# Routed experts on sorted tokens in blocks of 128 rows, in three of four chunks

## The chip, the cores and the metric

The kernel runs on one core of a Trainium2 chip. The metric is device time in microseconds (us) of one execution, all inputs in DRAM before and the output in DRAM after.

## The reference, cut to what matters

`x` is 16 sequences of 128 tokens of 128 features, `ctx` has the same shape. One decoder layer is computed in float32: 16-head self-attention with relative keys and values, causal cross-attention to `ctx`, and a mixture of experts, each followed by a residual add and a layer norm.

```python
x = _layernorm(x + _L0_attn_ref(x, ...))
x = _layernorm(x + _L0_xattn_ref(x, ctx_1024, ctx_1024, ...))
x = _layernorm(x + _L0_ffn_ref(x, ...))

def _L0_ffn_ref(hidden, router_w, router_b, sw1, sb1, sw2, sb2, rw1, rb1, rw2, rb2):
    flat = hidden.reshape(T, d)                                  # d = 128
    router_probs = jax.nn.softmax(flat @ router_w + router_b, axis=-1)     # 8 experts
    topk_probs, topk_idx = jax.lax.top_k(router_probs, 2)
    weights = jnp.zeros_like(router_probs).at[jnp.arange(T)[:, None], topk_idx].add(topk_probs)
    shared_out = jax.nn.gelu(flat @ sw1 + sb1, approximate=False) @ sw2 + sb2
    h1 = jax.nn.gelu(jnp.einsum('td,edh->teh', flat, rw1) + rb1[None], approximate=False)  # h = 256
    expert_out = jnp.einsum('teh,ehd->ted', h1, rw2) + rb2[None]
    mixed = jnp.einsum('ted,te->td', expert_out, weights)
    return (shared_out + mixed).reshape(b, s, d)
```

The weights are zero for all but 2 of 8 experts of a token, so three quarters of the routed products are multiplied by zero.

## The kernel before

The 16 sequences are taken in four chunks of 4, so a chunk is 512 tokens. For each chunk the work is cut into named steps: self-attention (`xT q k v bias p1 m p2 pv w2 pvT w2T X XT o ln`), cross-attention (`cT ck cv x1T cq c1 cm c2 cpv cpvT cX cXT co cln`), and the feed-forward part (`x2T r g up dn fln`). `st_` steps stack bf16 parts of queries and keys in SBUF by way of DRAM.

The order of all steps of all chunks is one list written out by hand in the text `SCHEDULE`. Every engine walks the same list and runs its own part of each step: TensorE (PE) the products, VectorE (DVE) and ScalarE (ACT) the reads from PSUM, GpSimd (POOL) the causal mask on the probabilities of `c2`, the residual bias and the `pow` of each layer norm, and SyncE (SP) the DMAs. Semaphores tie the engines together, so an engine that waits in one step holds back all its later steps. Steps of different chunks are interleaved: the feed-forward part of chunk 0 lies among the cross-attention of chunk 1 and the self-attention of chunk 2, and so on. The last chunk's feed-forward part has nothing beside it.

PSUM has two `ps_s` tiles of 128x1024 for scores and four `ps_f` tiles of 128x512 for all else, used in rotation. ACT computes both Exp (`p2`, `c2`, `r`) and Gelu (`up`); going from one to the other loads a table.

The feed-forward part is dense. `r` (L696, L993 to L1026) computes logits, softmax, and each expert's rank by a comparison of all pairs, and keeps the two highest as gate weights `gw`. `up` runs 18 times (9 experts, the shared one first, 2 halves of the hidden 256): one 512-column product from all tokens (L708), then Gelu on ACT (L833). `dn` runs 9 times: 8 products of 128 columns (L719), then DVE multiplies by the gate column and adds into `acc`, four instructions of 128x128 (L1044); the first `dn`, the shared expert's, adds `x2` and the output biases instead (L722, L1040). `fln` is the final layer norm and the store. All expert weights (2.1 MB) are loaded to SBUF at the start by `load_experts` (L374 to L386).

Of the kernel before, what the change touches and what calls it, by code (L numbers as in the profile page):

```python
# [15 lines left out]
BF16 = mybir.dt.bfloat16  # L16
ACT = mybir.ActivationFunctionType
# [23 lines left out]
NF = HID // P  # L41
NPC = 3
# [35 lines left out]
2xT 0cm.0 1pv.0 1p2.2 0c1.5 1p2.3 0c1.6 0c1.7 0c2.0 0cm.1 0c2.1 1p1.5 0c2.2 1pvT.0 1p1.6 0cpv.0 0c2.3 1pv.1
1p1.7 0cpvT.0 0c2.4 0cpv.1 0c2.5 1m.1 0c2.6 2q 2st_q 0c2.7 0cpv.2 1pvT.1 0cpvT.1 1p2.4 1p2.5 0cpvT.2 0cpv.3
1p2.6 1p2.7 1cv 2loadc 0cpvT.3 0cX 1pv.2 1ck 1w2.0 0cXT 2k 1w2.1 1pv.3 1w2.2 0co 0cln 1pvT.2 1w2.3 1pvT.3  # L80
2bias.0 1w2T.0 2bias.1 1w2T.1 1w2T.2 1w2T.3 1X 0x2T 2v 0r 1XT 2bias.2 2bias.3 1o 2bias.4 2bias.5 2st_k 0g
2bias.6 1ln 2bias.7 0up.0 2p1.0 0up.1 1x1T 2p1.1 0up.2 0up.3 1st_ck 3load 1cq 0up.4 0dn.0 2p1.2 0up.5 2p1.3
# [27 lines left out]


F_STEPS = {"xT", "q", "k", "v", "m", "pv", "w2", "pvT", "w2T", "XT", "o", "cT", "ck", "cv", "x1T", "cq", "cm",
           "cpv", "cpvT", "cXT", "co", "x2T", "r", "g", "up", "dn"}
# [969 lines left out]
```

## Time and profile before

| | us |
|---|---|
| median of 3 runs | 485.68 (484.39 to 485.95) |
| the profiled execution, whole | 484.97 |
| its span from first to last instruction | 482.9 |
| PE busy | 406.3 (84%) |
| DVE busy | 324.4 (67%) |
| ACT busy | 248.0 (51%) |
| POOL busy | 76.4 (16%) |

Busy time is the time in which an engine has an instruction in work; waits, and the issue of DMAs, are not in it. The granted clock is the share of 2.4 GHz that TensorE was given: 1.0 is 2.4 GHz, 0.5 is 1.2 GHz, and a mean between them is a mixture of the two in time. A float32 product appears as two matmul records.

### The profile page before, as it was taken

The numbers are of one execution on the slowest core, as the hardware profiler recorded it, in microseconds if no ns is written. First come the engines' busy times: TensorE is split into PE (matmuls) and PEld (weight loads), VectorE is DVE, ScalarE is ACT, GpSimd is POOL, SyncE is SP. The second block draws the span as 40 slices with busy tenths as digits, with TensorE's granted clock in tenths as the row PEclk, the third lists the DMA queues.
The fourth block names the chain that finished last, engine by engine and source line by source line (L and its number), as shares of the span: only waits on it lengthen the run. The fifth ranks groups of instructions, "written<-read, shape, count | busy, mean of one in ns | idle before, by whom it ended". The sixth has DMA issues, their size and how long they took to land.

```text
span 482.9 us, 11287 instructions
## 1 busy us (share of the span) xinstructions
PE 406.3 (84%) x4718; PEld 302.9 (63%) x4729; DVE 324.4 (67%) x630; ACT 248.0 (51%) x329; POOL 76.4 (16%) x84
## 2 busy tenths in 40 slices
PE   3775399847879999999899899998999998649992
PEld 2464158734656877767688676776786767525772
DVE  4429953698868787887787868888975377143233
ACT  2470187703558583368774932487973425514340
POOL 9700000201340120003411100113101102410000
PEclk9776589959999999999999999999999999876998
DMA  4558025140013513001121630011110200000001
GB/s 107 156 113 261 3 68 155 35 121 5 3 36 88 175 47 99 3 18 44 37 68 23 166 99 1 4 36 24 49 24 1 81 20 3 2 23 0 2 0 23
DMA packets 29324, 26.87 MB, mean 56 GB/s; under 512 B 12577, under 2 KB 27866, under 8 KB 28506
## 3 DMA queue, kind: packets, MB, share of 16 engines
q1 hardware_dynamic: 28442, 26.02, 20.0%
q8 instruction: 38, 0.62, 0.6%
q10 hardware_dynamic: 832, 0.13, 0.2%
q14 instruction: 12, 0.10, 0.1%
HBM read 18.38 MB, written 7.35 MB: 53 GB/s over the span
## 4 chain that ended last, share of the span: by engine, by line
PE 55%; DVE 22%; ACT 8%; DMA 5%; issue 4%; SPq 4%; POOL 1%; POOLq 0%; DVEq 0%; ACTq 0%
PE ps_f L708 12%; PE ps_f L719 11%; PE ps_s L545 8%; PE ps_f L571 5%; PE ps_f L671 3%; DVE ST L930 3%; DVE ST L960 3%; DMA QS<-MP 3%; PE ps_f L579 2%; ACT ST L786 2%; DVE MX L933 2%; PE ps_s L538 2%; PE ps_f L518 2%; PE ps_f L524 2%; SPq L414 2%
## 5 line engine op out<-in xcount | busy, mean ns | idle before, releaser
L545 PE MATMUL ps_s<-QS,KS 125*128 125x128 bf16 (+1 forms) x768 | 80.6, 249 | 16.7 <-DVE ST L930 11.2
L545 PEld LDWEIGHTS ps_s<-QS,KS 125*128 125x128 bf16 (+1 forms) x768 | 64.4, 106 | 43.9 <-issue 14.9
L833 ACT ACTIVATE HT<-ps_f,hb 128x512 f32<-128x512 f32 x72 | 48.9, 689 | 81.5 <-PE ps_f L708 39.2
L719 PEld LDWEIGHTS ps_f<-w,HT 128*128 128x128 f32 x576 | 69.2, 192 | 10.0 <-issue 7.4
L708 PE MATMUL ps_f<-x2T,w 128*128 128x512 f32 x144 | 73.5, 619 | 0.0
L719 PE MATMUL ps_f<-w,HT 128*128 128x128 f32 x576 | 73.3, 278 | 0.0
L790 ACT ACTIVATE ST<-ST 128x1024 f32<-128x1024 f32 x32 | 33.6, 1060 | 52.1 <-DVE ST L960 51.7
L1044 DVE SCALAR_TENSOR_TENSOR acc<-ps_f,gw,acc 128x128 f32<-128x128 f32 x128 | 37.4, 363 | 31.3 <-PE ps_f L719 31.2
L483 POOL TENSOR_SCALAR_AFFINE_SELECT PC<-PC 128x1024 f32<-128x1024 f32 x32 | 34.8, 1096 | 147.8 <-ACT PC L797 147.7
L930 DVE TENSOR_TENSOR ST<-ps_s,ST 128x1024 f32<-128x1024 f32 x32 | 38.6, 1207 | 13.4 <-PE ps_s L545 13.4
L937 DVE TRANSPOSE_TENSOR_REDUCE MX<-ps_s 128x32 f32<-128x1024 f32 x32 | 39.0, 1237 | 7.1 <-PE ps_s L545 7.1
L960 DVE TENSOR_TENSOR ST<-ps_s,ST 128x1024 f32<-128x1024 f32 x32 | 38.1, 1215 | 7.2 <-PE ps_s L554 7.0
L933 DVE TRANSPOSE_TENSOR_REDUCE MX<-ST 128x32 f32<-128x1024 f32 x32 | 39.8, 1245 | 1.1
L797 ACT ACTIVATE PC<-ps_s 128x1024 f32<-128x1024 f32 x32 | 32.5, 1026 | 14.2 <-PE ps_s L545 7.9
L489 POOL TENSOR_TENSOR ve<-mv,epst 128x4 f32<-128x4 f32 x12 | 2.4, 200 | 218.0 <-DVE mv L877 218.0
L708 PEld LDWEIGHTS ps_f<-x2T,w 128*128 128x128 f32 x144 | 25.0, 199 | 14.5 <-issue 13.5
L671 PE MATMUL ps_f<-ST,RV 128*8 128x64 f32 x1024 | 32.2, 290 | 0.1
L786 ACT COPY ST<-ps_s 128x1024 f32<-128x1024 f32 x32 | 30.6, 1028 | 3.0 <-PE ps_s L630 2.9
L671 PEld LDWEIGHTS ps_f<-ST,RV 128*8 128x8 f32 x1024 | 28.6, 107 | 3.7 <-issue 2.0
L554 PE MATMUL ps_s<-QS,onesr 128*128 128x512 bf16 x53 | 18.0, 415 | 14.5 <-DVE ST L930 5.1
L538 PE MATMUL ps_s<-maskT,identb 128*128 128x512 bf16 x64 | 26.1, 408 | 2.9 <-DMA QS<-parts_by_head 1.2
L805 ACT COPY OT<-ps_f 128x512 f32<-128x512 f32 x32 | 22.6, 709 | 7.7 <-PE ps_f L571 7.6
(114 smaller groups left out, 560.7 us busy)
## 6 DMA issues: line engine op xcount, KB each, us to landing
parts_by_head<-part SPq DMA_DIRECT2D x16, 384.0 KB, 2.7
QS<-parts_by_head SPq DMA_DIRECT2D x24, 256.0 KB, 3.8
KS<-parts_by_head SPq DMA_DIRECT2D x24, 256.0 KB, 4.9
xin<-in_x SPq DMA_DIRECT2D x16, 64.0 KB, 2.1
cin<-in_ctx SPq DMA_DIRECT2D x4, 256.0 KB, 4.5
w<-in_L_ffn_rw SPq DMA_DIRECT2D x1, 1024.0 KB
out_x<-acc SPq DMA_DIRECT2D x16, 64.0 KB, 1.8
QS<-MP SPq DMA_DIRECT2D x48, 8.0 KB, 2.1
```

What stands on the lines that cost most here:

```text
L538: nc.tensor.matmul(ps[:, half * BANK:(half + 1) * BANK], identb[:, :], maskT[:, :, :].broadcast_to([P, 4, S]), start=True, stop=False, ski ...
L545: last = nc.tensor.matmul(ps[:, o:o + S], KS[a][0:kd, c:c + S], queries(a, kd, h, j), start=not masked and j == 0, stop=j == NB - 1, skip_ ...
L671: last = nc.tensor.matmul(ps[a * QD:a * QD + HD, jj * HB:(jj + 1) * HB], RV[:, S - 1 - q, :], st_q[:, :, q, :], start=jj == 0, stop=jj == ...
L708: nc.tensor.matmul(ps[:, :], w1[:, e, f * P:(f + 1) * P], x2T[:, :], start=True, stop=True).then_inc(f_full, 1)
L719: last = nc.tensor.matmul(ps[:, b * E:(b + 1) * E], HT[n % 2][:, f, b * S:(b + 1) * S], w2[:, e, f, :], start=f == 0, stop=f == NF - 1 and ...
L786: nc.scalar.copy(dst, ps[:, :].rearrange("p (q c b) -> p c q b", q=nq, b=2)).then_inc(bias_ready, 1)
L833: nc.scalar.activation(HT[n % 2][:, f, :], ps[:, :], ACT.Gelu, bias=hb[:, e, f:f + 1]).then_inc(ht_ready, 1)
L930: nc.vector.tensor_tensor(by_bank(w), ps[:, :].rearrange("p (c b q) -> p c q b", b=2, q=S), by_bank(w), ALU.add).then_inc(sum_ready, 1)
L933: nc.vector.tensor_reduce(MX[0][:, t * 32:(t + 1) * 32], w.rearrange("p (c i) -> p c i", i=QD), AXIS.X, ALU.max, apply_transpose=True).the ...
L937: nc.vector.tensor_reduce(MX[1][:, t * 32:(t + 1) * 32], ps[:, :].rearrange("p (c i) -> p c i", i=QD), AXIS.X, ALU.max, apply_transpose=Tr ...
L960: nc.vector.tensor_tensor(w, ps[:, :], w, ALU.add).then_inc(sc_ready, 1)
L1044: last = nc.vector.scalar_tensor_tensor(acc[:, b, :], ps[:, b * E:(b + 1) * E], gw[ch % 2][:, b, t - 1:t], acc[:, b, :], ALU.mult, ALU.add)
```

## The change

In chunks 0, 1 and 2 the eight routed experts no longer see all tokens. After `r`, a new step `n` counts the tokens of each expert by products with a triangular and an all-ones matrix, and gives each of the 1,024 (token, choice) pairs a slot: experts lie one behind the other, each padded to whole blocks of 128 rows, 15 blocks in all (the most that can be needed). POOL scatters the rows of `x2` to these slots in a DRAM tensor, with 8 indirect DMAs of 128 rows (64 KB each). Then, for the 15 blocks, SP loads slots (`xs`, 4 per chunk, 4 blocks each), and the weights of the block's expert (`wl`, 15 per chunk, 128x514 values, 263 KB, at an address which SP reads from a table in SBUF; four buffers); PE transposes the rows (`xt`, 4), and runs `us` (8, for two blocks each: 2 products of 128 columns a block, then Gelu by 128x128 pieces, since the bias is the expert's) and `ds` (8: 2 products of 128 columns a block, then one copy to SBUF). SP stores the results (`ys`, 4), POOL gathers them back with 8 indirect DMAs (`ga`), and DVE adds them into `acc` with the gate weights (`cb`, 8 instructions). Of `up` and `dn` only the shared expert's two and one are left. Chunk 3 stays dense; its expert weights are loaded during the kernel (`3lw`) into the self-attention's stacks of queries and keys when these are done with.

In such a chunk 24 of PE's 27 steps `up` and `dn` are gone, and 21 steps `n`, `xt`, `us` and `ds` come in their place. The loads of the routed weights at the start are gone too; a copy of 1 MB from `x` to the slots tensor, DRAM to DRAM, stands there. The expert weights are given to the kernel as one array packed per expert. The order of all steps is new, also at the start: chunk 1's load, transposes and queries come later, and `0cT` stands ahead of `0q`.

```diff
-0load 1load 0xT 0q 0v 0k 0cT 0loadc 0st_q 0st_k 1xT 0ck 1q 0bias.0 0cv 0bias.1 0bias.2 0bias.3 0bias.4 0bias.5
...
-3cXT 3co 3cln 3x2T 3r 3up.0 3up.1 3up.2 3up.3 3g 3up.4 3dn.0 3up.5 3dn.1 3dn.2 3up.6 3up.7 3up.8 3up.9 3up.10
-3dn.3 3up.11 3dn.4 3up.12 3up.13 3dn.5 3dn.6 3up.14 3up.15 3up.16 3up.17 3dn.7 3dn.8 3fln
+0load 0xT 0cT 0loadc 0q 0st_q 0k 1load 0v 0st_k 0ck 0cv 0bias.0 0bias.1 0bias.2 0bias.3 0bias.4 0bias.5 0st_ck
...
+2x2T 3pvT.0 3p2.5 3p2.6 1ys.3 3p2.7 1ga 2r 2wl.0 3pv.1 3pv.2 3cv 3w2.0 3w2.1 2n 3ck 1cb 3st_ck 3w2.2 2wl.1 3w2.3
+3pvT.1 2wl.2 3pvT.2 2xs.0 3pv.3 3lw 3w2T.0 2wl.3 3w2T.1 3pvT.3 2xs.1 3w2T.2 3w2T.3 3X 2xs.2 3XT 2wl.4 2wl.5
+2up.0 3o 2xt.0 2us.0 3x1T 2us.1 3ln 3cq 2ds.0 2xt.1 2wl.6 2ds.1 2wl.7 2xt.2 2up.1 2us.2 3st_cq 2ds.2 2wl.8 2us.3
+3c1.0 2wl.9 2xs.3 3c1.1 2wl.10 2wl.11 2ds.3 3c1.2 2ys.0 3c1.3 3cm.0 3c1.4 3c1.5 2us.4 2us.5 3c1.6 2wl.12 3c2.0
+2ds.4 2g 2wl.13 2wl.14 2ys.1 3c2.1 2xt.3 3c1.7 2ds.5 3c2.2 2ys.2 3cm.1 3cpv.0 1fln 3c2.3 2us.6 2us.7 3c2.4 2ds.6
+3c2.5 3cpv.1 2ds.7 3cpvT.0 3c2.6 3c2.7 3cpv.2 3cpvT.1 3cpvT.2 3cpv.3 3cpvT.3 2ga 3cXT 3cX 3co 2dn.0 3x2T 3cln
+2cb 3r 3up.0 3up.1 2ys.3 3up.2 3up.3 3g 3up.4 2fln 3up.5 3up.6 3dn.0 3dn.1 3up.7 3dn.2 3dn.3 3up.8 3up.9 3up.10
...
 SP:
+            def load_expert(ch, n):
+                if n == 0:
+                    sp.wait_ge(eid_ready, ch + 1)
+                k = N_BLK * ch + n
+                if k >= NW:                                    # NW = 4 buffers
+                    c_, n_ = divmod(k - NW, N_BLK)
+                    done_f(sp, (c_, "ds", n_ // 2))
+                e = sp.value_load(eid[0:1, n:n + 1], min_val=0, max_val=NEXP - 1)
+                sp.dma_start(WB[k % NW][:, :], experts[bass.ds(e, 1), :, :].rearrange("o p w -> p (o w)")
+                             ).then_inc(ld_wb[k % NW], 16)
 POOL, at n and ga:
+                    g.wait_ge(slots_ready, ch + 1)
...
+                    for k in range(TOP_K * NB):
+                        nc.gpsimd.indirect_dma_start(slots_x, bass.IndirectOffsetOnAxis(ap=slot[ch % 2][:, k:k + 1], axis=0),
+                                                     x2[:, k % NB, :], None).then_inc(scattered, 16)
...
+                    for k in range(TOP_K * NB):
+                        nc.gpsimd.indirect_dma_start(XG[:, k // NB, k % NB, :], None, slots_y,
+                                                     bass.IndirectOffsetOnAxis(ap=slot[ch % 2][:, k:k + 1], axis=0)
+                                                     ).then_inc(gathered, 16)
 PE, at us:
+                    for i, n in enumerate(blocks_of(t)):
+                        k = N_BLK * ch + n
+                        for f in range(NF):
+                            o = (i * NF + f) * P
+                            last = nc.tensor.matmul(ps[:, o:o + P], WB[k % NW][:, f * P:(f + 1) * P],
+                                                    XST[t // 2 % 2][:, n % GRP * P:(n % GRP + 1) * P], start=True, stop=True)
 DVE, at r: 4 more instructions; at n: 13 of 8 to 120 elements a partition; at ds and cb:
+                    nc.vector.tensor_copy(YS[g_ % 2][:, o:o + n], ps[:, 0:n]).then_inc(ys_ready, 1)
...
+                            last = nc.vector.scalar_tensor_tensor(acc[:, b, :], XG[:, k, b, :], gate[ch % 2][:, k, b:b + 1],
+                                                                  acc[:, b, :], ALU.mult, ALU.add)
```

## Rows read from the trace of the kernel before

**Rows 1.** The page: busy tenths and granted clock in 40 slices of 12 us.

```profile
PE   3775399847879999999899899998999998649992
...
DVE  4429953698868787887787868888975377143233
...
PEclk9776589959999999999999999999999999876998
```

**Rows 2.** Busy time by stretch; the column names are the first line.

```profile
core 0: us, PE busy (x) PEld busy (x) DVE busy (x) ACT busy (x) POOL busy (x), PEclk, DMA share, GB/s
172.00:412.00 240.00, 231.33 (x2606) 175.10 (x2608) 182.10 (x371) 142.70 (x186) 35.21 (x38) 1.00 0.15 41
412.00:435.00 23.00, 12.08 (x160) 8.93 (x160) 7.50 (x31) 7.45 (x13) 6.76 (x8) 0.78 0.06 13
435.00:449.00 14.00, 13.77 (x47) 8.30 (x48) 4.28 (x14) 4.65 (x8) 0.00 (x0) 0.75 0.00 1
...
25.00:60.00 35.00, 19.14 (x207) 13.90 (x208) 25.89 (x33) 9.81 (x12) 0.00 (x0) 0.65 0.47 124
```

**Rows 3.** The chain of waits that ended last, in order of time: start us, us, what (xcount).

```profile
419.70 1.02 PE ps_f L579 x8
...
449.76 3.57 PE ps_f L719 x32
453.33 4.29 PE ps_f L708 x10
```

**Rows 4.** Groups of instructions, DVE: busy, mean ns of one, idle before.

```profile
L1044 DVE SCALAR_TENSOR_TENSOR acc<-ps_f,gw,acc 128x128 f32<-128x128 f32 x128 | 37.4, 363 | 31.3 <-PE ps_f L719 31.2
...
L944 DVE TENSOR_REDUCE NM<-ps_f 128x32 f32<-128x128 f32 x16 | 4.3, 271 | 2.0 <-PE ps_f L563 2.0
...
L1032 DVE COPY gwT<-ps_f 9x512 f32<-9x512 f32 x4 | 2.7, 668 | 3.0 <-PE ps_f L703 3.0
...
L1024 DVE TENSOR_REDUCE rank<-rest 128x32 f32<-128x256 f32 x4 | 1.7, 420 | 0.1
...
L993 DVE TENSOR_TENSOR lg<-ps_f,rb_row 128x32 f32<-128x32 f32 x4 | 0.8, 190 | 4.4 <-PE ps_f L696 4.4
```

**Rows 5.** The same view, ACT.

```profile
L833 ACT ACTIVATE HT<-ps_f,hb 128x512 f32<-128x512 f32 x72 | 48.9, 689 | 81.5 <-PE ps_f L708 39.2 <-PE ps_f L719 24.1 <-PE ps_f L722 17.6
...
L820 ACT COPY X<-ps_f 128x144 f32<-128x144 f32 x32 | 11.8, 380 | 4.0 <-PE ps_f L579 3.8
...
L833 ACT ACT_TABLE_LOAD x8 | 10.3, 1283 | 0.1
...
L762 ACT COPY x2T<-ps_f 128x512 f32<-128x512 f32 x4 | 2.4, 588 | 8.5 <-PE ps_f L513 8.5
```

**Rows 6.** DMA issues: KB each, median us from issue to landing.

```profile
xin<-in_x SPq DMA_DIRECT2D x16, 64.0 KB, 2.1
cin<-in_ctx SPq DMA_DIRECT2D x4, 256.0 KB, 4.5
...
QS<-MP SPq DMA_DIRECT2D x48, 8.0 KB, 2.1
```

**Rows 7.** The timeline, SP at the start: start us, us, instruction.

```profile
8.36 0.43 SPq L343 DMA_DIRECT2D cin<-in_ctx  x1
```

**Rows 8.** The timeline, PE at the start.

```profile
10.11 2.05 PE L518 MATMUL ps_f<-TR,wT 128*128 128x512 f32 x2 [0.83 <-ACT TR L759]
...
15.36 0.64 PE L513 MATMUL ps_f<-ident,cin 128*128 128x128 f32 x4
```

**Rows 9.** The timeline, POOL in the last 80 us.

```profile
420.91 1.09 POOL L483 TENSOR_SCALAR_AFFINE_SELECT PC<-PC 128x1024 f32<-128x1024 f32 x1 [0.97 <-ACT PC L797]
...
431.23 1.01 POOL L491 TENSOR_TENSOR rstd<-ve,halfm 128x4 f32<-128x4 f32 x1
```

**Rows 10.** The timeline, DVE in the last 80 us.

```profile
437.14 0.19 DVE L993 TENSOR_TENSOR lg<-ps_f,rb_row 128x32 f32<-128x32 f32 x1 [3.76 <-PE ps_f L696]
```

More of the change, by code:

```diff
@@ L41 @@
 NF = HID // P
+N_BLK = (TOP_K * T - NEXP) // P + NEXP
+N_PAIR = (N_BLK + 1) // 2
+GRP = 4
+N_GRP = (N_BLK + GRP - 1) // GRP
+NW = 4
+PACK = HID + HID + NF
+DENSE = (3,)
 NPC = 3
@@ L78 @@
[L78 to L82, printed above, removed]
@@ L150, in build @@
         rb_row = sb("rb_row", [P, NEXP])
-        hb = sb("hb", [P, NEXP + 1, NF])
+        hb = sb("hb", [P, NF])
         ob = sb("ob", [NEXP + 1, E])
-        w1 = sb("w1", [P, NEXP + 1, HID])
-        w2 = sb("w2", [P, NEXP + 1, NF, E])
+        w1 = sb("w1", [P, HID])
+        w2 = sb("w2", [P, NF, E])
+        WB = [sb(f"WB{i}", [P, PACK]) for i in range(NW)]
+        before = sb("before", [P, P], BF16)
+        allone = sb("allone", [P, P], BF16)
+        full = sb("full", [P, NEXP, NB])
+        bidx = sb("bidx", [P, N_BLK, NEXP])
         wr = sb("wr", [P, NEXP])
@@ L195, in build @@
         gwT = sb("gwT", [NEXP + 1, NB, P])
-        HT = [sb(f"HT{i}", [P, NF, T]) for i in range(2)]
+        w12d = QS[0][:, :].bitcast(F32).rearrange("p (e w) -> p e w", e=NEXP)
+        hbd = KS[0][:, 0:2 * NEXP * NF].bitcast(F32).rearrange("p (e f) -> p e f", e=NEXP)
+        HT = [sb("HT0", [P, NF, T]),
+              KS[0][:, BANK:BANK + 2 * NF * T].bitcast(F32).rearrange("p (f t) -> p f t", f=NF)]
+        HS = [sb(f"HS{i}", [P, 2, NF, P]) for i in range(2)]
+        XS = sb("XS", [P, 2, GRP * P])
+        XG = XS[:, :, :].rearrange("p r (b e) -> p r b e", b=NB)
+        XST = [sb(f"XST{i}", [P, GRP * P]) for i in range(2)]
+        YS = [sb(f"YS{i}", [P, GRP * P]) for i in range(2)]
+        sel = sb("sel", [P, NB, NEXP], BF16)
+        many = sb("many", [P, NEXP, NB])
+        nblk = sb("nblk", [P, NEXP])
+        nsum = sb("nsum", [P, NEXP, NEXP])
+        first = sb("first", [P, NEXP])
+        past = sb("past", [P, NEXP])
+        slotf = sb("slotf", [P, NB, NEXP])
+        pick = sb("pick", [P, TOP_K, NB, NEXP])
+        slotp = sb("slotp", [P, TOP_K, NB])
+        slot = [sb(f"slot{i}", [P, TOP_K * NB], U32) for i in range(2)]
+        which = sb("which", [P, N_BLK, NEXP])
+        whichs = sb("whichs", [P, N_BLK])
+        eid = sb("eid", [P, N_BLK], I32)
+        gpick = sb("gpick", [P, TOP_K, NB, NEXP])
+        gate = [sb(f"gate{i}", [P, TOP_K, NB]) for i in range(2)]
         wnat = OT[:, 0:8 * P].rearrange("p (w i) -> p w i", w=8)
@@ L266, in build @@
         dn_done = sem("dn_done")
+        ld_d = sem("ld_d")
+        n_pool = sem("n_pool")
+        sel_ready = sem("sel_ready")
+        n_step = sem("n_step")
+        slots_ready = sem("slots_ready")
+        eid_ready = sem("eid_ready")
+        gate_step = sem("gate_step")
+        xs_init = sem("xs_init")
+        scattered = sem("scattered")
+        ld_xs = [sem(f"ld_xs{i}") for i in range(2)]
+        ld_wb = [sem(f"ld_wb{i}") for i in range(NW)]
+        xst_ready = sem("xst_ready")
+        hs_ready = sem("hs_ready")
+        ys_ready = sem("ys_ready")
+        ys_stored = [sem(f"ys_stored{i}") for i in range(2)]
+        gathered = sem("gathered")
+        cb_step = sem("cb_step")
         stored = sem("stored")
@@ L464, in _ @@
             nc.gpsimd.tensor_copy(identb[:, :], ident[:, :]).then_inc(c_pool, 1)
+            nc.gpsimd.memset(allone[:, :], 1.0).then_inc(n_pool, 1)
+            g.wait_ge(n_pool, 1)
+            nc.gpsimd.affine_select(out=before[:, :], in_=allone[:, :], compare_op=ALU.is_gt, fill=0.0,
+                                    base=0, pattern=[[1, P]], channel_multiplier=-1).then_inc(n_pool, 1)
+            for j in range(NB):
+                nc.gpsimd.memset(full[:, :, j:j + 1], float(P * j)).then_inc(n_pool, 1)
+            for j in range(N_BLK):
+                nc.gpsimd.memset(bidx[:, j:j + 1, :], float(j)).then_inc(n_pool, 1)
+            g.wait_ge(n_pool, 2 + NB + N_BLK)
             g.wait_ge(c_pool, 9)
```

302 lines of the change are left out of this document (245 added, 57 removed).

## The prediction

> **What bounds the kernel now.** I read the page's slices first [rows 1]: PE is at nine tenths or more from slice 15 to slice 34, DVE mostly at seven or eight, and the granted clock is full there. The table by stretch [rows 2] sharpens this. From 172 to 412 us, which begins as chunk 0's feed-forward part does and ends with chunk 2's, PE is busy 231.3 of 240 us at a granted clock of 1.00, DVE 182.1, ACT 142.7, the DMA engines at 15%. So there PE sets the pace. All three feed-forward parts that the change touches lie in this stretch. Outside it the kernel waits: from 25 to 60 us DVE has most to do (25.9 of 35 us, PE 19.1 at clock 0.65), and from 412 us on chunk 3 is alone. Time taken from PE in the middle is therefore worth nearly its full size, until DVE or a latency takes over.
>
> **What goes from PE.** The unit prices come from the chain of waits in time [rows 3], since the mean durations of single matmul records overlap: 32 records of L719 (two `dn` steps) take 3.57 us, so 1.785 us a `dn` and 0.223 us for one float32 product of 128 columns; 10 records of L708 (five `up` steps) take 4.29 us, 0.858 us each. Eight routed experts cost a chunk 16 x 0.858 + 8 x 1.785 = 28.0 us.
>
> **What comes to PE.** 15 blocks of 4 products of 128 columns: 60 x 0.223 = 13.4 us. 15 transposes: 8 of them take 1.02 us [rows 3], so 1.9 us. The 8 products of `n` have at most 32 columns in bf16; at a product's 0.223 us or less each they cost 0 to 1.8 us, and I take 0.6, since they have a quarter of the columns and one record instead of two. Sum 15.9 us. A chunk saves 12.1 us of PE, three chunks 36.3 us. PE's work in the stretch falls from 231 to 195 us.
>
> **DVE.** Gone: 32 accumulates at 0.363 us [rows 4] = 11.6 us a chunk. New: 7.5 copies of 256 columns, between 0.271 us (128 columns read) and 0.668 us (512) [rows 4], say 0.41, so 3.1 us; 8 accumulates of `cb`, 2.9 us; 17 small instructions in `r` and `n`, between 0.190 and 0.420 us each [rows 4], say 0.22, so 3.7 us. Net -1.9 us a chunk, -5.7 in all. DVE therefore goes from 182 to about 176 us in a stretch that would be about 204 us long if all of PE's gain were kept: 87% busy. DVE had 76% before. Such a load, with only two `ps_s` tiles between PE and DVE, makes PE wait. Between 0 and 8 us; I take 4.
>
> **ACT.** Gone: 16 Gelus at 0.689 us = 11.0 us a chunk. New: 30 Gelus of 128 columns, for which the copy of 144 columns at 0.380 us is an upper bound [rows 5] and half of it a lower one: 5.7 to 11.4 us, I take 9; four copies near 0.588 us, 2.2 us. About nothing. The two lists change between Exp and Gelu 16 and 22 times; six more table loads at 1.283 us [rows 5] are 7.7 us of ACT. ACT stays under 160 us of 204, so it hides in its idle time: 0, or up to 7.7 us if each load falls where PE waits for a Gelu.
>
> **The latency of the weights.** SP may load blocks 2u+4 and 2u+5 only after `ds.u` has read the old ones. A load of 256 KB lands 4.5 us after its issue [rows 6], and its issue takes 0.43 us [rows 7]. The reading of the expert number from SBUF by SP is in no row: between 0 and 2.1 us (the smallest DMA's way, [rows 6]); I take 0.5, as it moves four bytes and no DMA engine, nearer to the 0.43 us that SP needs for an issue. So a pair lands 2 x 0.93 + 4.5 = 6.4 us after `ds.u`. Against it stands PE's work in the new list between `ds.u` and `us.u+2`, priced as above: 5.5 to 9.5 us in chunk 0, 9.2, 7.0, 13.1, 10.2, 4.5, 3.8 us in chunk 1, and 2.8, 3.2, 12.1, 7.8, 6.2, 3.0 us in chunk 2. What is lacking adds up to about 16 us; neighbouring pairs share their waits, and waits for Gelus also pass the time, so I take half: +8 us (0 to 16; if SP's read is 2.1 us a pair takes 9.6 us and 50 us are lacking in all). Behind a waiting load on SP stand the stack loads and the shifts of the maxima, and PE waits for those.
>
> **The latency of the slots.** After `n` on PE come 13 dependent small DVE steps (about 3.5 us), 8 scatters on POOL, 2.1 us until the last lands, and a slot load (0.43 + 4.5 us): 10.5 us plus 8 scatters, before `xt.0`. An indirect DMA is in no row. Its cost to POOL lies between an issue on SP, 0.43 us, and a complete trip of 64 KB, 2.1 us [rows 6, 7]; I take 1.1, between the two. Then 19.3 us are needed. The list has 11.2 to 11.5 us of PE work there in each chunk, and perhaps 5 us more pass as PE waits for DVE and for layer norms anyway. Missing: about 3 us a chunk, +9 us in all (0 to 16).
>
> The Trainium skill ("DMA: Bandwidth & Descriptors", the anatomy of a DMA from GpSimd) gives 2.0 us plus bytes over 436 GB/s for a DMA issued there, most of it completion and so open to overlap, and its rules for kernel authors say that below 64 KB one pays mostly overhead. The trace agrees for 64 KB from SP, with 2.1 us [rows 6]. If the eight did not overlap, an estimate by that page is 17.2 us for eight, where I have 8.8; this is the third case below.
>
> **Start and end.** `0cT` now stands ahead of `0q`, which began at 10.11 us, though `ctx` is issued at 8.36 and lands 4.5 us later [rows 7, 8]; part of these 3 us comes back in SP's queue. I take +2 us (0 to 3). At the end, `2ga` stands on POOL between the mask of `3c2.7` (over at 422.0) and the `pow` of `3co`, which began at 431.23 [rows 9]. Eight gathers of 1.1 us fit nearly exactly; at 2.1 us chunk 3 is 8 us late. `2cb` (2.9 us) lies on DVE ahead of `3r`, in a gap of 3.76 us [rows 10]. `2fln` and its store must be over before `3dn.0`. `2dn.0` fills a hole of PE in front of the stretch from 435 to 449 us where the clock is 0.75 [rows 2], which may give back 1 or 2 us. Together +1 us (-2 to +8). New traffic, 11.8 MB of weights and 9 MB of slots in some 225 us, puts about 90 GB/s on top of 41 [rows 2], which leaves the DMA engines room: 0.
>
> **Sum.** -36.3 + 4 + 0 + 8 + 9 + 2 + 1 = -12.3. From the profiled execution's 484.97 us this is 472.7; the median of the runs is 0.7 us higher, so the two serve alike. I round to 472.
>
> **The rivals.**
>
> All of PE's gain is kept: the latencies lie in chunks whose PE work waits for DVE anyway. For it: in the new list many scores of the next chunk stand between the steps. Against it: the three short covers in chunk 2. 484.97 - 36.3 + 2 + 4 = 455.
>
> The scatters and gathers don't overlap, at 2.1 us each: place, POOL at `n` and `ga`; 8 us more for each of three scatters (+24) on top of the 9, and +8 for `3co`: 472.7 + 32 = 505. It decides from about 1.5 us each, where three scatters and the last gather, 8 x 0.4 us more each, 12.8 us together, eat the gain. For it: each scatter writes rows of 512 bytes to DRAM, and POOL must read the offsets first. Against it: SP issues its DMAs at 0.43 us without waiting for their landing [rows 7].
>
> The weight loads hold SP: SP's read costs 2.1 us, 50 us of cover are lacking, and half of that, as above, is 25 us in place of 8: 490. The shifts stand late behind the loads. For it: such a read may have to complete before SP goes on, as a DMA's trip does. Against it: four bytes need no DMA engine.
>
> The change doesn't save what it says: 15 blocks are the fixed count whatever the router does, so the products are exactly 60, and this can't fail; I give it no chance.
>
> **Chances.** My forecast with its own spread (461 to 482) 0.50; the gain kept 0.17; POOL serial 0.20; SP held 0.13. A change under 0.3% (1.5 us) can't be told from none here. Faster: 0.49 + 0.17 + 0.03 of SP held, 0.69; same 0.06, from SP held and the edge of the forecast; slower 0.20 + 0.05, 0.25. The range reaches from the first rival to half way into the serial one: 454 to 493.
>
> **What would show it.** PE busy falls from 406 to about 370 us. DVE's falls by about 5. A scatter's time on POOL near 1.1 us; `xt.0` waits for the slot DMA some 3 us in each chunk; `us` waits for `WB` mostly in chunk 2. The tail from `3co` on is as long as before, about 54 us. I am wrong if PE's waits on DMA grow by more than 30 us in all, if DVE becomes the engine that PE waits for from 172 us on by more than 10 us, or if the clock falls to its lower level in the middle.

## The result, and the profile after

The changed kernel takes 509.01 us (median of 4 runs, 505.92 to 510.47), the kernel before 485.03 (4 runs, 481.12 to 485.95). The ratio is 1.050, with a 95% interval of 1.042 to 1.058: 24 us slower, where 472 was predicted. The profiled execution took 510.38 us, with a span of 508.1 us. Medians in us are of all runs; ratios and their intervals leave out the runs that are over 1.5% slower than the quickest of their kernel.

The page of the changed kernel: busy time by engine, the slices (12.7 us each), the chain that ended last, and the two largest new DMA rows.

```profile
PE 386.5 (76%) x4678; PEld 300.2 (59%) x4678; DVE 316.3 (62%) x633; ACT 249.3 (49%) x389; POOL 126.3 (25%) x153
...
PE   1664597756899776999996769897863779669993
...
PEclk9985599959999896999999879998895779997897
DMA  4357006030004555442037635412159454210000
...
PE 41%; DVE 22%; DMA 13%; issue 7%; ACT 7%; SPq 6%; POOL 3%; POOLq 0%; DVEq 0%; ACTq 0%
...
WB<-in_experts SPq DMA_DIRECT2D x45, 257.0 KB, 3.1
...
QS<-in_experts SPq DMA_DIRECT2D x1, 2048.0 KB, 8.8
```

PE has less to do than before (386.5 us beside 406.3) and idles more (121.6 us beside 76.6). Its row of eights and nines [rows 1] has holes, and the granted clock has fallen below full in most of the same places.

The same by stretch, after; the column names are those of [rows 2].

```profile
175.00:265.00 90.00, 79.41 (x1059) 64.11 (x1056) 65.48 (x108) 61.74 (x97) 21.06 (x22) 0.94 0.38 106
265.00:353.00 88.00, 71.09 (x777) 58.62 (x776) 66.10 (x149) 51.26 (x84) 30.52 (x32) 0.92 0.48 125
353.00:457.00 104.00, 72.10 (x899) 58.23 (x897) 49.45 (x121) 41.89 (x77) 37.81 (x39) 0.87 0.43 120
457.00:509.00 52.00, 40.93 (x204) 28.74 (x204) 20.36 (x78) 14.35 (x21) 2.40 (x4) 0.84 0.04 11
```

And before, in the same kind of stretches:

```profile
175.00:265.00 90.00, 87.49 (x1038) 66.66 (x1039) 71.50 (x127) 55.39 (x74) 14.87 (x16) 1.00 0.16 42
265.00:353.00 88.00, 83.86 (x964) 63.70 (x966) 72.40 (x139) 57.42 (x74) 12.33 (x13) 1.00 0.19 52
353.00:434.00 81.00, 68.81 (x711) 51.34 (x711) 42.84 (x123) 34.03 (x49) 14.75 (x17) 0.94 0.09 23
```

From 175 to 353 us PE loses 20.9 us of work and hardly any time is won: chunk 2's `x2T` starts at 351.2 us, before at 352.9. Behind it the changed kernel falls back. The table shows where a step starts on PE (us; the step's first product in the timeline of PE; `c1` begins with the product that writes the mask, and "last dn" is read off the last 16 records of products):

```
                         x2T ch0  x2T ch1  x2T ch2  o ch3   c1 ch3  x2T ch3  last dn
before                    166.6    264.5    352.9   366.3   390.4   433.4    472.4
after                     165.0    267.6    351.2   378.4   411.8   456.9    497.6
h_oldnone                 164.3    251.8    331.9   345.1   365.3   407.5    445.3
i_newnone                 167.4    259.0    332.5   359.1   380.1   424.4    465.0
e_nolat                   164.1    264.6    345.4   372.4   395.6   441.2    481.9
q_stcq                    165.7    271.3    353.1   380.1   401.9   466.9    506.3
```

(The four lower lines are experiments, told below.) One distance stands out: from chunk 2's `x2T` to chunk 3's `o` PE takes 13 us in both kernels with the list of before, and 27 us in all four with the new list, with sorted work or without. In the new list `3p2.5` to `3p2.7`, `3pv.1`, `3pv.2`, `3cv`, `3w2.0`, `3w2.1` and `3ck` stand behind `2x2T`; in the old one they stand ahead of it.

What PE waited for in the changed kernel: us in total, times, longest.

```profile
PE ps_f L873 <- DMA XS<-slots_x: 13.9, 3, 5.9
PE ps_s L777 <- issue: 9.6, 4, 4.5
PE ps_s L692 <- DVE ST L1148: 9.1, 7, 2.3
PE ps_f L885 <- DMA WB<-in_experts: 7.3, 4, 3.8
```

The waits that the prediction named, for slots and for expert weights, are there with 21.2 us in all. Chunk 2's path to its first slots, in the chain in order of time (start us, us, what):

```profile
366.70 1.47 DVE which L1290
...
368.49 1.00 POOL slots_x L607
369.48 0.30 issue
...
377.54 4.96 DMA slots_x<-x,slot
382.52 0.38 SPq L474
382.95 0.50 SPq L461
383.50 0.58 SPq L462
...
384.83 8.78 DMA WB<-in_experts
```

Eight scatters on POOL from 368.5 us, the last landed at 382.5, then the slot load; behind it on SP stands the 2 MB read for chunk 3 (L461), and behind that an expert load that takes 8.8 us.

### The profile page after: what moved, and what is told of

Its sections match the earlier page's. It is cut to its first block, busy times and chain, and to the rows that moved or that the text cites. A ratio compares the mean times of both kernels' runs of the same rounds, so it can differ in the third digit from the quotient of the medians.

```text
span 508.1 us, 11680 instructions
## 1 busy us (share of the span) xinstructions
PE 386.5 (76%) x4678; PEld 300.2 (59%) x4678; DVE 316.3 (62%) x633; ACT 249.3 (49%) x389; POOL 126.3 (25%) x153
## 4 chain that ended last, share of the span: by engine, by line
PE 41%; DVE 22%; DMA 13%; issue 7%; ACT 7%; SPq 6%; POOL 3%; POOLq 0%; DVEq 0%; ACTq 0%
PE ps_s L692 6%; PE ps_f L914 5%; PE ps_f L904 4%; PE ps_f L718 4%; PE ps_f L894 3%; DVE ST L1178 3%; DMA QS<-MP 3%; PE ps_f L885 3%; POOL slots_x L607 3%; DMA WB<-in_experts 3%; DVE MX L1155 2%; DVE ST L1148 2%; PE ps_f L665 2%; DVE MX L1151 2%; PE ps_f L726 2%
## 5 line engine op out<-in xcount | busy, mean ns | idle before, releaser
L1050 ACT ACTIVATE HS<-ps_f,WB 128x128 f32<-128x128 f32 x90 | 25.5, 371 | 40.2 <-PE ps_f L885 40.1
L885 PE MATMUL ps_f<-XST,WB 128*128 128x128 f32 x180 | 29.4, 314 | 9.1 <-DMA WB<-in_experts 7.3
L885 PEld LDWEIGHTS ps_f<-XST,WB 128*128 128x128 f32 x180 | 26.0, 222 | 12.0 <-issue 10.9
L777 PE MATMUL ps_s<-QS,RK 125*128 125x64 bf16 x512 | 21.7, 200 | 14.7 <-issue 9.6
L818 PEld LDWEIGHTS ps_f<-ST,RV 128*8 128x8 f32 x1024 | 27.3, 106 | 7.1 <-issue 5.4
L1127 DVE SCALAR_TENSOR_TENSOR rest<-ps_f,bcol,part 128x512 f32<-128x512 f32 x16 | 12.2, 762 | 30.7 <-ACT part L971 30.0
L818 PE MATMUL ps_f<-ST,RV 128*8 128x64 f32 x1024 | 30.1, 283 | 0.9 <-DVE rest L1127 0.9
L777 PEld LDWEIGHTS ps_s<-QS,RK 125*128 125x128 bf16 x512 | 19.0, 103 | 17.5 <-issue 10.1
L894 PE MATMUL ps_f<-WB,HS 128*128 128x128 f32 x180 | 27.9, 303 | 1.2 <-ACT HS L1050 1.2
L614 POOL DMA_INDIRECT XS<-slots_y,slot x24 | 24.3, 1013 | 15.1 <-DMA slots_y<-YS 8.6
```

Of the source, the lines that this page charges most:

```text
L777: last = nc.tensor.matmul(ps[:, j * HB:(j + 1) * HB], RK[0:KZ, S - 1 - q:2 * S - 1 - q], qs_q[:, :, q, :], start=True, stop=True)
L818: last = nc.tensor.matmul(ps[a * QD:a * QD + HD, jj * HB:(jj + 1) * HB], RV[:, S - 1 - q, :], st_q[:, :, q, :], start=jj == 0, stop=jj == ...
L885: last = nc.tensor.matmul(ps[:, o:o + P], WB[k % NW][:, f * P:(f + 1) * P], XST[t // 2 % 2][:, n % GRP * P:(n % GRP + 1) * P], start=True, ...
L894: last = nc.tensor.matmul(ps[:, i * P:(i + 1) * P], HS[(N_PAIR * ch + t) % 2][:, i, f, :], WB[k % NW][:, HID + f * P:HID + (f + 1) * P], s ...
```

## The experiments

All against the kernel before on the same chip; its median lay between 481.7 and 484.1 us in these runs, and was 485.0 beside the changed kernel. Medians of 4 to 10 runs; one kernel's runs lie up to 16 us apart, and a difference of two medians can shift by some 3 us if it is taken between the ratios instead. So a few us between two kernels don't count.

### Is it the new list or the new data path?

**a_order**: dense experts in all four chunks, but in the new list, each `us.t` replaced by two `up` and each `ds.t` by a `dn`.

```diff
- 2p1.4 0us.0 0wl.4 0xt.1 1c1.0 1c1.1 0ds.0 0us.1
+ 2p1.4 0up.2 0up.3 1c1.0 1c1.1 0g 0dn.0 0dn.1 0up.4 0up.5
```

> The old dense computation in all four chunks, in the new kernel's order: each us of the new list is replaced by the two up of one expert, each ds by that expert's dn; g and dn.0 stand ahead of them and fln right behind the last dn of its chunk; nothing of slots, scatters, gathers or expert loads is left. Order theory (the new list itself is worse): 495 to 510 us. Latency theory (the list is fine, the new round trips make PE wait): 482 to 490, like the kernel before. Traffic theory: the same 482 to 490.

547.1 us (ratio 1.136, 1.125 to 1.147), further off than any of the three theories had it. With the same list the sorted path is 38 us better than the dense one (41 by the ratios), about the 36 predicted for PE, with its latencies included; but the list is made for short feed-forward parts and says little of what it costs them.

**f_oldorder**: the sorted path in the list of before, its steps delayed by 12 to 14 places; the scatters are a step of their own, chunk 3 adds into another buffer, and the 2 MB read stands behind `3p2.7`.

```diff
- 2p1.4 0up.8 1st_cq 0dn.2 0up.9 0up.10 2m.0 1c1.0
+ 2p1.4 0us.0 1st_cq 2m.0 0us.1 1c1.0 1c1.1 1c1.2 2p2.0 0ds.0 0wl.4 0wl.5
```

> Sorted experts in the first three chunks, put into the list of the kernel before: its steps keep their order, the steps n, xt, us, ds, ga, cb take the places of the dense up and dn, delayed by 12 to 14 places so that the slots have landed; the scatters are a step of their own, chunk 3 accumulates in another buffer (it need not wait for chunk 2's end), 3lw behind 3p2.7. Theory 'order' (the new list itself is what loses: it lost 62 us on dense work): 455 to 475. Theory 'latency and loads' (what loses are the slot round trip, the expert reads and the lower clock behind their stalls, whatever the list): 490 to 505.

579.3 us (ratio 1.195, 1.186 to 1.205), far outside both. What PE waited for:

```profile
PE ps_s L692 <- DMA KS<-parts_by_head: 24.1, 1, 24.1
PE ps_f L873 <- DMA XS<-slots_x: 22.7, 3, 13.7
PE ps_f L885 <- DMA WB<-in_experts: 15.9, 8, 5.7
```

One stack load of the attention came 24.1 us late, at 321.9 us. SP takes its items in order. In front of this load stood the store of a finished chunk, which waited 13.8 us for the final layer norm on DVE, and four expert loads, the first of which waited 4.9 us for the expert numbers. So this list loses more than everything in question here, and the run doesn't tell the two theories apart: whether a list near the old one could carry the sorted path well stays untested.

### What is a microsecond of PE worth?

This is the pair that says most. **h_oldnone**: the kernel before, its list kept, without the routed experts of chunks 0 to 2. **i_newnone**: the changed kernel without any sorted step; the work of h_oldnone in the new list, plus the 2 MB read.

```diff
# h_oldnone
- 2bias.7 0up.0 2p1.0 0up.1 1x1T 2p1.1 0up.2 0up.3 1st_ck 3load 1cq 0up.4 0dn.0 2p1.2 0up.5 2p1.3 0up.6 0dn.1
+ 2bias.7 0up.0 2p1.0 0up.1 1x1T 2p1.1 1st_ck 3load 1cq 0dn.0 2p1.2 2p1.3
# i_newnone
- 2p1.4 0us.0 0wl.4 0xt.1 1c1.0 1c1.1 0ds.0 0us.1 2p2.0
+ 2p1.4 1c1.0 1c1.1 2p2.0
```

> The kernel before, its list kept, with the routed experts of chunks 0 to 2 left out altogether (48 of its 72 up products and 24 of its 36 dn products with their gelus and sums; the shared expert stays, chunk 3 is whole). It leaves out 3 x 28.0 = 84 us of TensorE work by the count of the prediction. Theory 'PE is the bound' (the premise of the sum: a saving on TensorE comes back one to one in the middle): 395 to 415. Theory 'the attention chain is the bound' (once the products shrink, the softmax chain over VectorE, ScalarE, the masks and the shifts sets the pace, about 88 us a chunk, and the products only fill it): 440 to 465, so that no form of routed experts could have gained much more than 20 to 45.

> The changed kernel, its list kept, with every sorted step of chunks 0 to 2 left out (counting, scatter, slot loads, expert loads, products, stores, gathers, sums); the same work as in the kernel before without its routed experts, but in the new list, and the 2 MB read for chunk 3. Theory 'order' (the new list costs by itself): 15 us or more above that kernel. Theory 'latency' (the list is as good, only what was inserted stalls): within 8 us of it, and 45 us or more under the changed kernel.

460.5 us (ratio 0.954, 0.948 to 0.961) and 481.2 us (0.995, 0.991 to 0.999). Leaving out 84 us of counted PE work altogether, and DVE's and ACT's part of it, brings 24 us: 0.28 us for each, as a mean. No form of routed experts in these three chunks, however cheap, could have gained more in this list. What the first 36 us alone would have brought wasn't measured: at most these 24. By stretch, h_oldnone:

```profile
175.00:265.00 90.00, 74.52 (x1025) 55.62 (x1024) 70.98 (x124) 49.87 (x67) 15.05 (x17) 0.92 0.23 61
265.00:353.00 88.00, 68.67 (x893) 50.79 (x894) 66.25 (x118) 38.28 (x51) 14.71 (x16) 0.94 0.12 32
```

The chain that ended last in h_oldnone, from its page:

```profile
PE 35%; DVE 33%; DMA 11%; ACT 7%; issue 6%; SPq 5%; POOL 1%; POOLq 0%; DVEq 0%; ACTq 0%
```

And what PE waited for most in it:

```profile
PE ps_s L535 <- DMA QS<-parts_by_head: 16.9, 3, 11.1
PE ps_s L542 <- DMA QS<-MP: 13.0, 6, 3.3
PE ps_s L542 <- DVE ST L927: 11.4, 11, 1.9
```

No engine is full there (PE 143.2 and DVE 137.2 of 178 us). What is left is mainly the attention's own chain: projections through DRAM into the stacks, scores, maxima on DVE, shifts by DMA, softmax. That this chain sets the pace is read from these rows and wasn't tested apart. The distance between two `x2T` is 87.5, 80.1 and 75.6 us, and was 97.9, 88.4 and 80.5 with 28 us of routed products in each: 10, 8 and 5 us more for 28. The clock is 0.92 and 0.94 in place of 1.00, and PE's busy time fell by 67.4 us, not 84. The routed products were in large part filling for waits that stay when they go: PE waits for DMA 48.6 us in h_oldnone, and 17.1 in the kernel before.

i_newnone is 21 us above h_oldnone (20 by the ratios). So the new list, with the read that belongs to it, costs some 20 us on the work that both kernels share. By the table nearly all of it arises behind chunk 2's `x2T` (332.5 beside 331.9 us there, 359.1 beside 345.1 at chunk 3's `o`, 424.4 beside 407.5 at its `x2T`): 13 us of it between chunk 2's `x2T` and chunk 3's `o`, where the new list has more of chunk 3's self-attention still to do.

### What does the sorted path cost on top?

**c_aside**: the scatters write to a tensor that nobody reads, and the slot loads don't wait for them. **d_norel**: only the first 4 of 45 expert loads. **e_nolat**: both, and the 2 MB read behind `2wl.14`.

```diff
# c_aside
-    sp.wait_ge(scattered, 16 * TOP_K * NB * (ch + 1))
+    sp.wait_ge(xs_init, 16)
-    nc.gpsimd.indirect_dma_start(slots_x, ...
+    nc.gpsimd.indirect_dma_start(slots_a, ...
# d_norel, in load_expert
     if k >= NW:
-        c_, n_ = divmod(k - NW, N_BLK)
-        done_f(sp, (c_, "ds", n_ // 2))
+        return
```

> The scatters go to a DRAM tensor that nobody reads, the slot loads read the tensor as it was filled at the start and no longer wait for the scatters: the values are wrong, the bytes, instructions and order are the same. Latency theory: the 13.9 us that PE waits for slots at xt go, and some 5 us of lower clock behind them: 488 to 495 us. Traffic theory and order theory: 504 to 510.

> Only the first four of the 45 expert loads are made, and the blocks use whatever four weights lie in the buffers: 10.8 MB less traffic, 41 fewer issues and register reads on SP, no wait for a freed weight buffer. Latency theory: PE's waits for WB (7.3 us) and what stands behind SP's waits there (about 8 us) and some clock go: 490 to 498 us. Traffic theory: also the stack loads and shifts speed up, 480 to 488. Order theory: 505 to 510.

> The changed kernel, its list kept but 3lw behind 2wl.14; the scatters go to a tensor that nobody reads and the slot loads don't wait for them, and only the first 4 of 45 expert reads are made, so the experts' products use stale rows and weights. Leaves out the sorting's effect and 41 expert reads; all of PE's, VectorE's and ScalarE's work stays. Theory 'latency': no round trip and no expert reads left, 470 to 485. Theory 'order': the two parts gave 4 and 8 us alone, 495 to 502.

504.9 us (1.051, 1.044 to 1.059), 501.6 (1.035, 1.024 to 1.046) and 496.6 (1.028, 1.019 to 1.036). c_aside misses what the latency theory said of it (488 to 495), and by its ratio it can't be told from the changed kernel; d_norel lies between its theories; e_nolat is where the order theory had it. Without the wait for the scatters and without the loads the changed kernel is still some 13 us slower than the one before. But the slot loads themselves stayed, behind the attention's stack loads in SP's order, and PE still waits for them:

```profile
PE ps_f L873 <- DMA XS<-slots_x: 9.5, 3, 5.2
PE ps_f L872 <- DMA XS<-slots_x: 6.5, 3, 3.1
```

(c_aside and e_nolat; 13.9 us in the changed kernel.) So these runs bound what the scatters' way costs and not all of the slots' latency. What stays above i_newnone, 15 us, goes with 45 us of products, transposes and counting on PE (386.5 less 341.6 us of busy time in the changed kernel and i_newnone) and with those 6.5 us of waits.

**k_noind**: the 48 indirect DMAs left out, their waits turned to the slot numbers and the loads.

```diff
-    nc.gpsimd.indirect_dma_start(slots_x, ..., x2[:, k % NB, :], None).then_inc(scattered, 16)
+    pass
```

> The changed kernel with its 48 indirect DMAs left out (24 scatters, 24 gathers), and the waits for them turned to the slot numbers and the loads; slot loads, expert loads and products stay (on stale rows). Theory 'indirect DMAs cost' (1.26 us each in a row on GpSimd, 10 us of the round trip twice a chunk, and VectorE some 1 us slower for each instruction beside them): 482 to 496. Theory 'off the path' (no more than the 4 us of the loads that didn't wait): 500 to 508.

508.2 us (502.9 to 516.6), not to be told from the changed kernel. The scatters' 10 us in each chunk's round trip and 48.3 us of POOL are gone, and the median hasn't moved. Its two quickest runs, 502.9 and 505.3, leave room for some 5 us, not for the 13 to 27 of the first theory. PE still waits 7.9 us for slot loads here.

### The 2 MB read

**b_lw** moves it behind `2wl.14`, **b2_early** right behind `3p2.7`, **p_split** cuts it into eight of 256 KB, and **l_nonesplit** does this in i_newnone.

```diff
# b2_early
- 3p2.5 3p2.6 1ys.3 3p2.7 1ga ... 3pv.3 3lw 3w2T.0
+ 3p2.5 3p2.6 1ys.3 3p2.7 3lw 1ga ... 3pv.3 3w2T.0
# p_split, l_nonesplit
-    sp.dma_start(w12d, experts[:, :, 0:2 * HID].rearrange("e p w -> p e w"))
+    sp.dma_start(w12d[:, t, :], experts[t, :, 0:2 * HID])
```

> Only 3lw, the 2 MB load of chunk 3's dense weights, is moved from behind 3pv.3 to behind 2wl.14 in the list. Latency theory with its special case (this load stands ahead of the slot and expert loads of chunk 2; one issue behind it took 4.3 us and 2us.1 waited 3.8 us): 500 to 504 us, and the wait of 2us.1 is gone. Order theory and traffic theory (the same bytes): 507 to 510.

> The changed kernel with the 2 MB read of chunk 3's dense expert weights (3lw) moved forward in the list, right behind 3p2.7: ahead of chunk 2's slot and expert loads instead of among them. Theory 'collision' (the read costs what stands behind it on the queues, so it should stand where nothing small is due): the 3.8 us wait at 2us.1 and the 4.33 us issue behind it go and no shift is held, 499 to 504. Rival 'it costs some 10 us wherever it stands' (seen when it was moved back: 3c1.0 came 10 us earlier and the end none): 507 to 513.

> The changed kernel, whole, its list kept, with the same eight reads of 256 KB in place of the one of 2 MB. Theory 'read': 498 to 502, as with the whole read moved forward (501.1). Rival: eight reads among 45 expert reads and their waits only spread the cost, 504 to 510.

> The new list without any sorted step (as i_newnone, so it leaves out the routed experts of chunks 0 to 2), with the 2 MB read of chunk 3's dense weights cut into eight of 256 KB, put one by one between 3p2.7 and 3c1.0. Theory 'read' (the one large read holds the spread and the stacks of chunk 3 behind it, 9.3 us longest wait for the mask rows): 468 to 474. Theory 'list' (the order of the steps costs it): 478 to 483.

b_lw: 513.0 us (1.067, 1.056 to 1.077), above both expectations. Chunk 3's `c1` comes 10 us sooner, at 401.3, but its shifts now stand behind the read:

```profile
PE ps_s L692 <- DMA QS<-MP: 10.1, 3, 8.5
```

b2_early: 501.1 us (1.032, 1.022 to 1.042), the fastest whole version of the changed kernel, as the collision theory had it: its place in the list was worth 8 us. p_split: 507.8 us (1.052, 1.045 to 1.059), as its rival said: no gain by cutting and spreading. l_nonesplit: 481.6 us (0.994, 0.990 to 0.999), the same as i_newnone: cutting and spreading the read wins nothing of the new list's cost back.

### Clock, start and SyncE's order

**g_fill**: 96 matmuls of no use where PE waits for slots and experts: 16 at each chunk's `xt.0`, as shown, and 12 at each of `2us.1` to `2us.4`.

```diff
+    ps = take_f(pe, s)
+    if t == 0:
+        fill(ps, 16)
     pe.wait_ge(ld_xs[t % 2], ...)
-    ps = take_f(pe, s)
```

> The changed kernel with matmuls of no use put on TensorE where it waits: 16 of 128 x 512 (bf16, about 0.22 us each) ahead of each chunk's first transpose of slots (xt.0), 12 ahead of each of 2us.1 to 2us.4; 96 in all, some 21 us of work at full clock. Theory 'clock' (half of what the stalls cost is the lower clock behind them, the granted clock was 0.51 to 0.70 in the 10 us behind a stall): the useful work behind the stalls runs at full clock, the time doesn't rise, 498 to 510. Theory 'PE is full' (no effect of the clock; the dummies are longer than the waits that they fill): 513 to 530.

515.1 us (1.068, 1.058 to 1.078), 6 us more than the changed kernel. The number lies in the second theory's range, but that theory had no effect of the clock, and there is one. The stretches behind the stalls, first in the changed kernel, then in g_fill:

```profile
190.00:200.00 10.00, 6.17 (x38) 5.00 (x37) 5.84 (x10) 2.20 (x6) 1.62 (x2) 0.58 0.69 185
...
385.00:405.00 20.00, 12.37 (x52) 9.74 (x52) 2.20 (x4) 6.50 (x15) 1.26 (x1) 0.63 0.64 186
```

```profile
190.00:200.00 10.00, 7.83 (x42) 4.90 (x43) 4.91 (x9) 0.89 (x3) 1.93 (x2) 0.83 0.66 186
385.00:405.00 20.00, 16.37 (x90) 11.42 (x91) 2.11 (x4) 7.35 (x19) 1.26 (x1) 0.91 0.79 233
```

The granted clock rises from 0.58 to 0.83 and from 0.63 to 0.91 (1.00 is 2.4 GHz, 0.5 is 1.2 GHz; a mean between them is time at either), in stretches that hold the filling too. PE's busy time is 404.1 us with at least 21 us of filling in it (the 16 at 192.4 us took 4.92), so the useful work took at least 3 us less. A better clock behind the stalls didn't pay for filling them here.

**j_hybrid** takes the list of before up to `0r`, with the read as in b2_early. **q_stcq** (on top of p_split) puts each `st_cq` in front of the slot and expert loads on SP and mixes `3c1.0` to `3c1.3` with chunk 2's first products. **r_qold** does both.

```diff
# q_stcq
- 3lw.4 3X 2xs.2 3XT 2wl.4 2wl.5 2up.0 3o 3lw.5 2xt.0 2us.0 3x1T 2us.1 3ln 3cq 3lw.6 2ds.0 2xt.1 2wl.6 ... 3st_cq
+ 3lw.4 3X 3XT 3lw.5 2up.0 3o 3ln 3x1T 3cq 3st_cq 3lw.6 2xt.0 2us.0 2xs.2 2wl.4 2wl.5 2us.1 3c1.0 2ds.0 2xt.1 2wl.6 3c1.1
```

> The changed kernel with the list of the kernel before up to chunk 0's router step (0r), then the new list without the steps already done, and 3lw right behind 3p2.7. At 0r chunk 1's o stood at 170.5 us in the kernel before and at 173.8 in the new list. Theory 'order': the 3 us stay, 495 to 500. Rival: the sorted path's waits swallow them, as they did the products' saving, 500 to 504.

> The kernel of the eight reads, with SyncE's order changed: each chunk's st_cq (the stack of cross-attention's q) stands right behind cq, ahead of the slot and expert loads that wait for the sorting, and chunk 3's c1.0 to c1.3 are mixed with chunk 2's first sorted products rather than behind them. Theory 'SyncE held' (in the changed kernel chunk 3's c1 starts 23 us behind its x1T, where the kernel before takes 15 and the one without routed experts 3): c1 of chunk 3 at 395 or before, 488 to 496. Rival 'chain' (what is won at c1 is lost to the products that now come later): 498 to 503.

> The same with the list of the kernel before up to chunk 0's router step. Theory 'order at the start': 2 to 4 us below the kernel with the moved st_cq. Rival: the same time within 2 us, as it was without the moves (504.7 beside 501.1).

504.7 us (1.044, 1.037 to 1.051), 520.7 (1.083, 1.073 to 1.092) and 518.8 (1.071, 1.061 to 1.081). j_hybrid lies at the edge of its rival's range; q_stcq is above both of its own. There chunk 3's `c1` started at 401.9 us, 10 us sooner than in the changed kernel but not at 395, and its `x2T` at 466.9, 10 us later: 65 us from one to the other, where the changed kernel takes 45 and h_oldnone 42. (The expectation's 3 us from `x1T` to `c1` without routed experts is wrong: in h_oldnone they are at 350.9 and 365.3, and 11.1 us of that is a wait for a stack load.) What the steps wait for between `c1` and `x2T` wasn't followed further. None of these beats the kernel before, and no version that would was found.

## Why the prediction was wrong

**The step that failed** is the conclusion of its first part: "Time taken from PE in the middle is therefore worth nearly its full size, until DVE or a latency takes over." In the list of before, all of the routed products, 84 us as counted, were worth 24 us (h_oldnone). So a saving of 36.3 us could bring 24 at most there; in proportion it would be 10, an estimate. PE's 96% [rows 2] was no reserve that could be cashed in full: the list had put products where the attention chain leaves PE free. The reading of the slices behind it was a little off as well: of slices 15 to 34 of PE five are eights, not nines [rows 1].

The same rows had the warning. Beside PE's 231.3 us stand 175.1 of 240 us of weight loads, 73% [rows 2]. The Trainium skill ("Perfetto Trace Analysis", Identifying the Most-Contended Engine) says that the matmuls' busy share is a poor measure of how near TensorE is to its limit, and that the weight loads' share is to be used beside a count of the work done. The trace agrees in direction only: the share of weight loads is 73% where the matmuls' is 96%, and the saving was worth far less than its size.

**The order was not in the sum at all.** The list was taken only as the cover for latencies. On equal work it costs some 20 us without routed experts (i_newnone less h_oldnone), and 63 to 65 us with dense ones (a_order less the kernel before). Single edits to it moved the time by -8 (b2_early) to +13 us (q_stcq over p_split).

**A ledger that closes** (medians): 484 us before; -24 without the dense products of three chunks (h_oldnone 460.5); +21 for the new list and its 2 MB read (i_newnone 481.2); +15 for the sorted path's work (e_nolat 496.6); +12 for the scatters' way, the expert loads and the read's place: 509.0. By the ratios the four steps are -22, +20, +16 and +11. It holds in this order of steps only. In the other order it reads: +63 for the new list with dense work (a_order 547.1), -38 for the sorted path in it, 509.0. There the swap of products is worth its predicted 36, and the list is the whole loss. Both are true, since a microsecond of PE has no fixed worth: in the new list the first 45 us of products cost 15, and the 84 us of the dense ones cost 66. What doesn't depend on the order of steps is that no swap of products could bring more than 24 us from 485 in the old list, and that the new list lost at least 20.

Point by point:

- PE's prices were right for what came: the sorted path added 44.9 us of busy time in three chunks, 15.0 a chunk, predicted 15.9. What went took only 67.4 us of busy time with it, not 84. This is the reason that total PE busy is 386.5, not 370; the work that stayed ran in stretches at a lower granted clock (0.94, 0.92 and 0.87 in the changed kernel, before 1.00, 1.00 and 0.94).
- The clock was named as a sign of being wrong and given no price. It did fall in the middle, to 0.58 and 0.63 in the stretches above, behind stalls of PE; in g_fill it rose again and the time didn't fall.
- The two other signs: PE's waits on DMA grew from 17.1 to 46.8 us in all, just under the 30 that were set, and its waits on DVE from 172 us on from 7.6 to 18.0, just over the 10. The first sign wouldn't have found the cause: h_oldnone, faster than the kernel before, has 48.6 us of waits on DMA.
- DVE: busy time fell by 8.1 us, predicted 5.7; what its coupling to PE cost wasn't measured apart.
- ACT: 22 table loads were predicted and 22 are there (7, 5, 5, 4 and 1). Busy 249.3 us, as before.
- Slots: needed in chunk 2 from `n` (363.4) to the landing (385.4) 22 us, predicted 19.3. A scatter holds POOL for 1.00 us, and 0.30 us lie between two, predicted 1.1:

```profile
L614 POOL DMA_INDIRECT XS<-slots_y,slot x24 | 24.3, 1013 | 15.1 <-DMA slots_y<-YS 8.6 <-issue 6.6
L607 POOL DMA_INDIRECT slots_x<-x,slot x24 | 24.0, 999 | 10.7 <-issue 6.4 <-DVE slot L1293 4.3
```

  the last one lands 4.96 us after it begins, where 2.1 were set. PE waited 13.9 us, predicted 9; c_aside took 4.4 us of this wait away and gained 4 us by the medians, none by the ratios.
- The serial rival (505) came near in its number and not in its mechanism: eight scatters take 10.0 us on POOL (368.49 to 378.51), not 17.2 as they would one by one. The Trainium skill ("DMA: Bandwidth & Descriptors", Anatomy of one DMA) says that most of a DMA's fixed 2.0 us is completion. The trace agrees that the pieces overlap, at 1.3 us each on POOL with the landings behind; but the last one's 4.96 us are more than the page's 2.0 us plus its 64 KB, and the measurement decides. k_noind, without them, gained at most some 5 us.
- Expert loads: SP's read of a number is about 0.7 us (the closest loads stand 1.07 to 1.15 us apart, of which 0.36 is the issue), predicted 0.5; a load landed in 3.1 us (median), where 4.5 were set. PE waited 7.3 us for `WB`, predicted 8, and leaving the loads out gave 7.4. So a read costs a third of the 2.1 us that the rival of the held SP had set.
- Traffic was put at 0. It is 96 GB/s over the span; what this mean costs no run shows apart. But one read of 2 MB held an expert load for 8.8 us, or a shift for 8.5, by where it stood (8 us between b2_early and the changed kernel).
- Start: `0c1.0` at 108.9 us, before 105.4, +3.5 (predicted 2); with the start of the old list in j_hybrid nothing was gained at the end (504.7 beside b2_early's 501.1). The tail from chunk 3's `x2T` is 51 us, before 49.5: as predicted.

So the 37 us between 472 and 509, by the first ledger: 27 for the swap of products (-24 + 15 = -9 in place of -36.3), 21 for the list, and -12 for the other terms, for which 24 us were set and 12 measured. The unit prices of the new work were good to a few us; what they were multiplied with was not.

Open: why the new list costs what it does. Its start and the form of the read are not likely to be the main part, by j_hybrid (which has the sorted work in it) and l_nonesplit. The table puts 13 of the 20 us between chunk 2's `x2T` and chunk 3's `o`. No run moved chunk 3's `p2`, `pv` and `w2` steps back ahead of `2x2T`, and that would be the test; q_stcq changed the order behind `3o` only, and lost.

## What to carry to other kernels

An engine that is 96% busy in a kernel whose order was fitted to it may tell only that its idle time has been filled, and not that its work sets the time. An engine's time has no fixed worth per microsecond. Before a rewrite is costed, leave the work in question out altogether and measure: that one run (460.5 us) bounds every version of it in the same order of steps. Here it would have shown that a saving of 36 us can bring 24 at most, and a second such run in the new order that this order loses 20. Where queues are taken in order, a new data path brings its waits into the queue of everything else; cost the order as a part of its own, with the new work taken out.

## What the runs showed of the hardware

Some instructions of DVE that read and write SBUF take several times as long as the same line elsewhere. Chunk 2 of the changed kernel, timeline:

```profile
358.71 3.57 PE L818 MATMUL ps_f<-ST,RV 128*8 128x64 f32 x128
...
360.58 1.45 DVE L1242 TENSOR_TENSOR rest<-rest,tri 128x256 f32<-128x256 f32 x1
361.41 1.38 POOL L614 DMA_INDIRECT XS<-slots_y,slot  x1 [0.30 <-issue]
...
362.54 0.42 DVE L1246 TENSOR_REDUCE rank<-rest 128x32 f32<-128x256 f32 x1
```

and chunk 1:

```profile
271.95 1.19 POOL L614 DMA_INDIRECT XS<-slots_y,slot  x1 [0.30 <-issue]
...
272.35 0.42 DVE L1242 TENSOR_TENSOR rest<-rest,tri 128x256 f32<-128x256 f32 x1
```

1.45 beside 0.42 us for the same line. POOL, with its indirect DMAs, is the neighbour that one would suspect. The Trainium skill ("SBUF — State Buffer", Terms) says that DVE and GpSimd share a pair of ports that one holds for a whole instruction while the other is blocked. But the rows don't bear it out for this case: in chunk 1 POOL issues an indirect DMA at the same time and the line takes 0.42 us, and in k_noind, where POOL is idle and issues none, the same line (L1232 there) takes 0.94 us in chunk 2, and the one ahead of it 1.41 where 0.42 is usual:

```profile
355.32 3.45 PE L809 MATMUL ps_f<-ST,RV 128*8 128x64 f32 x128
355.43 1.41 DVE L1229 TENSOR_TENSOR rest<-prob 128x256 f32<-128x256 f32 x1
356.87 0.94 DVE L1232 TENSOR_TENSOR rest<-rest,tri 128x256 f32<-128x256 f32 x1
```

i_newnone, which has no indirect DMA either, shows 1.98 and 1.51 us for these two lines. What the long rows have in common is PE: they lie beside a run of 128 records of `w2`'s small products (358.71 to 362.28 us here, 355.32 to 358.77 in k_noind, 340.62 to 344.40 in i_newnone). Why they are long is open; no run tested it. The expectation for k_noind, that VectorE is slower beside the indirect DMAs, is wrong by the same rows.
